# A graph network layer on one core: the first stage's weight centring moved to ScalarE, and pair sums of 17 edge chunks moved to GpSimd

## The reference

```python
xn = layernorm(x)
# graph part: sum, max and mean of the edges of each destination
out1 = segment_sum(edge_attr, dst);  out2 = segment_max(edge_attr, dst);  out3 = out1 / max(cnt, 1)
g = relu(concat([xn, out1, out2, out3, u]) @ W1 + b1) @ W2 + b2 + xn
# linear attention
q, k, v = split(xn @ W_qkv + b_qkv, 3)
q = q - mean(q);  k = k - mean(k)
k2 = l2norm_over_nodes(k*k / (sum(k*k) + 1e-7));  q2 = l2norm(q*q / (sum(q*q) + 1e-7))
m = (v + q2 @ (k2^T v) / sqrt(N)) @ W_out + b_out
x = x + g + m
# last network on the half of the nodes with the largest router weight
x = x + scatter(idx, (gelu(xs @ w1 + fb1) @ w2 + fb2) * w_sel) + layernorm(x)
```

## Time and profile before

| | |
|---|---|
| median of three runs | 1211.26 us (1210.34 to 1219.01) |
| the profiled execution's own time | 1217.11 us |
| its span, from first to last instruction | 1215.4 us |
| TensorE's mean granted clock over the span | 0.917 of full |
| VectorE busy over the span | 1011.2 us, 83% |
| TensorE busy over the span | 1062.9 us, 87% |
| GpSimd busy over the span | 465.4 us, 38% |

### The profile page before, as it was taken

The page is one execution under the profiler, slowest core; times in us unless marked ns, Lnnn a source line. Parts: engine busy times, 40 slices in busy tenths (PEclk is TensorE's granted clock), DMA queues, the critical chain, the costliest instruction groups (busy, mean ns, idle before and its releaser), DMA issues.

```text
span 1215.4 us, 15786 instructions
## 1 busy us (share of the span) xinstructions
PE 1062.9 (87%) x4570; PEld 763.7 (63%) x4570; DVE 1011.2 (83%) x2419; ACT 482.8 (40%) x1421; POOL 465.4 (38%) x341
## 2 busy tenths in 40 slices
PE   3198999999998367769999999999999967799996
PEld 1044555555554245447888888888888863588885
DVE  6899999999999999847988888988888566566672
ACT  3345777567762124412332233332233331333430
POOL 0078850888300002367565444565441000223411
PEclk9588999999997679869999999999999985699997
DMA  9879999999997899652443332443331130111100
GB/s 313 309 276 349 354 359 355 345 364 349 356 322 297 301 397 390 248 163 73 139 150 119 127 130 82 150 143 123 124 115 50 47 112 0 36 38 47 55 23 20
DMA packets 96013, 235.53 MB, mean 194 GB/s; under 512 B 13703, under 2 KB 68764, under 8 KB 89682
## 3 DMA queue, kind: packets, MB, share of 16 engines
q1 hardware_dynamic: 49890, 156.61, 35.0%
q10 hardware_dynamic: 31248, 44.71, 10.3%
q0 software_dynamic: 14816, 33.53, 9.9%
HBM read 154.25 MB, written 80.55 MB: 193 GB/s over the span
## 4 chain that ended last, share of the span: by engine, by line
PE 49%; POOL 3%; DVE 3%; issue 2%; DMA 1%; another core or an unknown queue 0%; ACT 0%; DVEq 0%; POOLq 0%
PE psR L67 5%; PE psC L67 5%; PE psQ L56 5%; PE psQ L57 5%; PE psKx L57 5%; PE psQ L58 5%; PE psKx L56 5%; PE psKx L58 5%; PE psR L68 3%; PE psC L68 2%; POOL graw L460 2%; PE psT L2012 1%; POOL grow L485 1%; PE psQ L2033 1%; PE psKx L2033 1%
## 5 line engine op out<-in xcount | busy, mean ns | idle before, releaser
L460 POOL DMA_INDIRECT graw<-in_edge_attr,ic x98 | 143.4, 1464 | 74.8 <-DVE ob L966 39.2
L963 DVE SCALAR_TENSOR_TENSOR ob<-ob,mQ,mx 128x96 f32<-128x96 f32 x392 | 122.3, 312 | 4.7 <-issue 0.4
L966 DVE SCALAR_TENSOR_TENSOR ob<-ob,kQ,xb 128x96 f32<-128x96 f32 x392 | 122.0, 311 | 0.0
L635 POOL DMA_INDIRECT near<-ends_d,blki x49 | 89.2, 1821 | 76.8 <-DVEq L872 62.2
L635 POOL DMA_INDIRECT near<-in_dst,rowi x49 | 87.8, 1792 | 57.8 <-DVEq L881 43.1
L1692 ACT ACTIVATE hT_hi<-psQ 128x512 fp32r<-128x512 f32 (+1 forms) x52 | 29.8, 574 | 185.0 <-PE psQ L2033 160.4
L1834 PE MATMUL psQ<-Wqk,xT 128*128 128x512 f32 (+1 forms) x196 | 102.3, 646 | 0.0
L951 DVE TENSOR_TENSOR xb<-xb 128x1536 f32<-128x1536 f32 x49 | 86.1, 1758 | 1.7
L949 DVE TENSOR_TENSOR mx<-xb 128x1536 f32<-128x1536 f32 x49 | 85.5, 1746 | 0.9
L729 POOL DMA_INDIRECT out_x<-zo,lst x25 | 24.4, 977 | 113.3 <-DVE zo L1384 113.3
L1692 ACT ACTIVATE hT_hi<-psKx 128x512 fp32r<-128x512 f32 (+1 forms) x52 | 29.7, 573 | 91.6 <-PE psKx L2033 83.8
(11 more groups left out here) (497 smaller groups left out, 3234.5 us busy)
## 6 DMA issues: line engine op xcount, KB each, us to landing
xb<-in_edge_attr SPq DMA_DIRECT2D x49, 1536.0 KB
scan_d<-ob SPq DMA_DIRECT2D x49, 768.0 KB
yrow_d<-yr SPq DMA_DIRECT2D x48, 132.0 KB
xg<-in_x ACTq DMA_DIRECT2D x12, 512.0 KB
xT_d<-xT ACTq DMA_DIRECT2D x12, 512.0 KB
base_d<-dcur ACTq DMA_DIRECT2D x12, 512.0 KB
qT_d<-qT ACTq DMA_DIRECT2D x12, 512.0 KB
out_x<-xres SPq DMA_DIRECT2D x48, 128.0 KB
```

What stands on the lines that cost most here:

```text
L460: nc.gpsimd.indirect_dma_start(out=to.rearrange("p i f -> p (i f)"), out_offset=None, in_=raw_v, in_offset=bass.IndirectOffsetOnAxis(ap=ic ...
L635: nc.gpsimd.indirect_dma_start(out=near[:, t, :], out_offset=None, in_=table, in_offset=bass.IndirectOffsetOnAxis(ap=rows[:, t:t + 1], axi ...
L963: nc.vector.scalar_tensor_tensor(o[:, q, 0:EF], prev[:, 0:EF], mQ[:, bass.ds(c * TQ + q, 1)], mx[:, q, 0, :], ALU.min, ALU.max).then_inc(s ...
L966: nc.vector.scalar_tensor_tensor(o[:, q, EF:AGG], prev[:, EF:AGG], kQ[:, bass.ds(c * TQ + q, 1)], X[:, q, 0, :], ALU.mult, ALU.add).then_i ...
```

## The change

Three things are changed together.

1. **Centring on ScalarE.** `centre_weights` on VectorE is gone. ScalarE does it with 12 activations: six that make minus the mean through an accumulator, six that add it. VectorE keeps the splitting (`query_bias`), now ahead of `variances`; `bias_row` stands behind chunk 0. `bqs`, `brow` and `one_r` have 128 partitions, cleared by GpSimd, and the bias matmuls have 128 rows in place of 2.
2. **Pair sums on GpSimd.** For chunks 30 to 46 (`PAIRS`) the pair sums are made by GpSimd (`pair_sums`), each when the chunk's pair maxima are done. VectorE makes the pair maxima of chunk c+1 inside chunk c, behind a wait for that chunk's load.
3. **Places.** `NORM` has smaller chunk numbers, the attention's factors come after chunk 35 in place of 39, `ends_of_segments` after 38 in place of 39, the graph network's weights are loaded from chunk 39 in place of 40. The product of `Eend` stands behind the fourth attention group; the tail parts, and ScalarE's `weights(GROUPS)`, stand later.

In the diff `pair_sums` is in GpSimd's list, `pair_maxima` and the lines on `PAIRS` after it in VectorE's, the loop over `centred` in ScalarE's.

```diff
+            PAIRS = range(30, 47)
+            def quarters(b):
+                return xb[b][:, :, :, :].rearrange("p q (h two) f -> p q h two f", two=2)
...
+                def pair_sums(chunks):
+                    for c in chunks:
+                        xp = quarters(c % XB)
+                        pool.wait_ge(s_tree, TREE[c, "max1"])
+                        nc.gpsimd.tensor_tensor(xp[:, :, :, 0, :], xp[:, :, :, 0, :], xp[:, :, :, 1, :], ALU.add).then_inc(s_pair, 1)
+                pair_sums(range(PAIRS[0], 44))
                 pool.wait_ge(s_idx, 1)
...
+                pair_sums(range(44, PAIRS[-1] + 1))
                 early(0, s_g0r)
...
+                def pair_maxima(c):
+                    xp = quarters(c % XB)
+                    dve.wait_ge(s_load[c % XB], c // XB * 16 + 16)
+                    if c in PAIRS:
+                        dve.wait_ge(s_max, (c - 1) * TQ + 1)
+                    nc.vector.tensor_tensor(mxs[c % 2][:, :, :, :], xp[:, :, :, 0, :], xp[:, :, :, 1, :], ALU.max).then_inc(s_tree, 1)
...
+                    if c not in PAIRS:
+                        xp = quarters(b)
+                        pair_maxima(c)
+                        dve.wait_ge(s_tree, TREE[c, "max1"])
+                        nc.vector.tensor_tensor(xp[:, :, :, 0, :], xp[:, :, :, 0, :], xp[:, :, :, 1, :], ALU.add).then_inc(s_tree, 1)
+                    if c + 1 in PAIRS:
+                        pair_maxima(c + 1)
...
+                    if c in PAIRS:
+                        dve.wait_ge(s_pair, c - PAIRS[0] + 1)
...
-                NORM = {5: 0, 7: 1, 10: 2, 13: 3, 16: 4, 18: 5, 21: 6, 24: 7, 26: 8, 29: 9, 32: 10, 34: 11, 35: 12}
+                NORM = {4: 0, 6: 1, 9: 2, 11: 3, 14: 4, 16: 5, 19: 6, 21: 7, 24: 8, 26: 9, 29: 10, 32: 11, 33: 12}
...
+                act.wait_ge(s_wload, 16 * 8)
+                for w_, m_, o_ in centred:
+                    nc.scalar.activation(o_, w_, ACT.Copy, scale=-1.0 / NF, accum_out=m_).then_inc(s_cw, 1)
+                for i, (w_, m_, o_) in enumerate(centred):
+                    act.wait_ge(s_cw, i + 1)
+                    nc.scalar.activation(w_, w_, ACT.Identity, bias=m_).then_inc(s_cw, 1)
+                act.wait_ge(s_bw, 2)
+                act.dma_start(brow[1:2, :].bitcast(f32), brow_l[0:1, :].bitcast(f32)).then_inc(s_row, 16)
+                act.wait_ge(s_wq, 1)
+                act.dma_start(bqs[1:2, :].bitcast(f32), bqs_l[0:1, :].bitcast(f32)).then_inc(s_row, 16)
                 act.wait_ge(s_ln, 1)
                 nc.scalar.sqrt(sd[:, :], va[:, :]).then_inc(s_sqrt, 1)
...
-                    nc.tensor.matmul(o, one_r[0:2, 0:rows], bqs[0:2, :], start=True, stop=False)
+                    nc.tensor.matmul(o, one_r[:, 0:rows], bqs[:, :], start=True, stop=False)
```

More of the change, by code:

```diff
@@ L354, in build @@
             s_xs = [sem(f"s_xs{i}") for i in range(4)]
-            s_run = sem("s_run")
-            s_diag = sem("s_diag")
+            s_cw = sem("s_cw")
+            s_pair = sem("s_pair")
             s_ct = sem("s_ct")
@@ L455, in build @@
                     9: ("h5", "l8", "l9"), 10: ("l10", "l11"), 12: ("t0", "t1", "t2", "t3")}
+            PAIRS = range(30, 47)
+            TREE = {}
+            for c_ in range(CHUNKS):
+                own = () if c_ in PAIRS else ((c_, "max1"), (c_, "add1"))
+                ahead = ((c_ + 1, "max1"),) if c_ + 1 in PAIRS else ()
+                for k_ in own + ahead + ((c_, "max2"), (c_, "add2")):
+                    TREE[k_] = len(TREE) + 1
+            def quarters(b):
+                return xb[b][:, :, :, :].rearrange("p q (h two) f -> p q h two f", two=2)
             def gather_raw(e, nt, rows, done):
@@ L800, in row_ends, with query_bias @@
                     dve.sem_inc(s_cbc, 1)
[L802 to L820, removed]
+                def query_bias():
+                    dve.wait_ge(s_cw, 12)
+                    dve.wait_ge(s_id, 9)
                     step(nc.vector.tensor_copy(one_r[0:2, :], ones[0:2, :]), False)
@@ L981, in _ @@
                 edge_chunk(0, 0, 0)
+                bias_row()
                 stats_quarter(1)
                 stats_quarter(2)
+                stats(GROUPS, 1, LAST, xs[0], s_xs[0], 64)
+                query_bias()
                 variances()
-                centre_weights()
-                bias_row()
                 deviations()
@@ L1653, in attention_rows @@
                         fetch(g + 4)
-                for g in range(GROUPS + 1):
+                for g in range(GROUPS):
                     attention_rows(g, g % 4, g // 4 * 16)
                     weights(g)
+                attention_rows(GROUPS, 0, GROUPS // 4 * 16)
                 for e in range(4):
@@ L1843, in base @@
                     o = psC[0:rows, 0:NF]
-                    nc.tensor.matmul(o, one_r[0:2, 0:rows], brow[0:2, :], start=True, stop=False)
+                    nc.tensor.matmul(o, one_r[:, 0:rows], brow[:, :], start=True, stop=False)
                     for c in range(KF):
@@ L1933, in _, with starts_of_segments @@
                 ins.then_inc(s_pt, 1)
-                pe.wait_ge(s_end, 1)
-                nc.tensor.matmul(psR[:, 0:TILES], shift[:, :], Eend[:, :], start=True, stop=False)
-                nc.tensor.matmul(psR[:, 1:TILES], corner[:, :], Eend[:, 0:TILES - 1], start=False, stop=True).then_inc(s_t, 1)
                 pe.wait_ge(s_at, 6 + KF)
+                def starts_of_segments():
+                    pe.wait_ge(s_end, 1)
+                    nc.tensor.matmul(psKx[1][:, 0:TILES], shift[:, :], Eend[:, :], start=True, stop=False)
+                    nc.tensor.matmul(psKx[1][:, 1:TILES], corner[:, :], Eend[:, 0:TILES - 1], start=False, stop=True).then_inc(s_t, 1)
                 def low_part(i):
@@ L1945, in low_part @@
                     pe.wait_ge(s_min, 4)
+                    if i == 3:
+                        pe.wait_ge(s_idx, 1)
                     if i >= 4:
@@ L1981, in _ @@
                     attention(g, g % 4, g // 4 * 16 + 16)
+                    if g == 3:
+                        starts_of_segments()
                     weights(g)
@@ L1994, in _ @@
                 ins.then_inc(s_t, 1)
-                tail_part(2)
-                tail_part(3)
+                for i in range(4):
+                    tail_part(i)
                 def node_stage():
```

63 lines of the change are left out of this document (28 added, 35 removed).

## The result

The kernel before took 1215.04 us (median of 4 runs), the changed one 1234.37 us (1229.56 to 1236.35): the ratio is 1.015, with an interval from 1.0111 to 1.0189. A second comparison of the same two kernels on another occasion gave 1.0161 (1.0133 to 1.0188), 1234.19 us against 1214.13. The change makes the kernel some 19 us slower. A few executions in this document were far longer whatever the kernel (1389.2 us for the kernel before, 1373.5 in experiment 1, 3494 and 5585 in experiment 6), and the ratios leave them out.

What follows compares the result with a forecast made beforehand. VectorE bounds the scan, busy 178.68 of 182.82 us from chunk 30 on. Pair sums +27, start -3 and key norms +2 made +26 us on a median of 1211.3: 1237 us, range 1226 to 1251.

Steps and rivals of the forecast that it cites:

- the side that had 0.87: Whole kernel: the change makes it slower by over 1%, chance 0.87.
- Both engines at one time: Scan: VectorE's two-SBUF-input instructions and a reading GpSimd instruction exclude each other; what GpSimd takes, VectorE loses.
- rival (a): Pair sums in the scan: the engines share after all, scan steps keep their usual length, 1184 us; chance 8%.
- Part 1, +27 us: Pair sums on GpSimd: 3.3 us lost, 1.7 freed, net +1.6 us a chunk over 17 chunks.
- Rival (b): GpSimd's pair sums: addition dearer on runs of 96 elements, 4.2 us each, 12 us more, 1249 us; chance 13%.
- Rival (d): GpSimd's pair sums: addition cheaper or partly beside one-input instructions, 0.5 us less a chunk, 1228 us; chance 8%.
- Part 2, -3.2 us: Start of the scan: with centring on ScalarE, chunk 1 starts at 51.6 us and not 54.8.
- this path ends last: Start of the scan: ScalarE's DMA issue, table load and root end at 49.5 us, later than the variances at 48.85.
- Part 3, the key norms, +2 us: Earlier key norms: VectorE might wait for ScalarE's squares, bounds 0 and 7 us, taken as +2.
- cost no more columns: Bias matmuls with 128 rows: no added columns; could bring TensorE's clock, up to 3.4 us gained each time.
- waits don't add: Key norms: VectorE waits 7 us ahead of group 9's norm, less for other groups, without summing.
- Rival (c): Key norms in the scan: they wait in full, +5 us more, 1242 us; chance 14%.

Runs made afterwards that it cites:

- experiment 1: The changed kernel with all pair sums on VectorE again and no pair maxima ahead: 1209.08 us, ratio 0.9953 to the kernel before.
- experiment 6: The changed kernel with GpSimd's pair sums in chunks 30 to 37 alone, 8 in place of 17: 1221.96 us, ratio 1.0067 to the kernel before.
- experiments 3: The changed kernel with GpSimd clearing the 1536 elements in place of adding them, pair sums left out: 1189.53 us in one execution.
- Experiment 4: The changed kernel with GpSimd adding two flat halves of the chunk in place of every second run of 96: 1232.63 us in one execution.
- experiment 5: The changed kernel with GpSimd copying the 1536 elements (one SBUF input) in place of adding two: 1200.24 us in one execution.
- experiment 10: The changed kernel with all pair sums on VectorE and ScalarE's table load early, right behind the centring: 1205.87 us in one execution.
- experiment 9: The changed kernel with all pair sums on VectorE and bias products of 2 rows, not 128: 1217.66 us, ratio 1.0021 to the kernel before.
- experiment 2: The kernel before with only the pair sums of chunks 30 to 46 on GpSimd and pair maxima ahead: 1237.39 us, ratio 1.0196.

## Why the prediction was right, and where it was not

The forecast was 1237 us with a range of 1226 to 1251, and the time was 1234.4, on the side that had 0.87. That it came out within 3 us is partly luck, since two errors offset each other: it stood on a median of 1211.3 for the kernel before, which more runs put at 1214 to 1216, and its sum of +26 was +19.5 (1.0161 x 1214 less 1214).

- **Both engines at one time.** Right in kind: experiments 3, 4 and 5 show that VectorE's two-input instructions wait for a GpSimd instruction that reads, and not for one that only writes. So rival (a) falls. The Trainium skill's rule in "SBUF — State Buffer", section "Who interferes with whom", says the same of reading and writing, and the traces agree (0.95 us for L970 under a clear, 4.20 under an addition).
- **Part 1, +27 us.** It was +22.5. Of the two figures in it, the loss of 3.3 us a chunk was 3.1 (3.25 and 3.0 in the two patterns), and the 1.7 us freed were 1.8. The prediction had both patterns, except that it saw the second as a wait of VectorE for the sums; in fact a scan step is held. Both errors go one way, 0.28 us a chunk: that is the term that was mis-sized. Most of it comes from the length of the addition, 3.5 us in the prediction (2.2 ns an element) and 3.3 in the trace, once it has its turn.
- **Rival (b), runs of 96 elements.** Experiment 4: no difference. Rival (d), 0.5 us less a chunk, is nearest to what happened, at a little over half its size.
- **Part 2, -3.2 us.** 29.5 and 30.2 us against 32.6 and 32.5: -2.7 on average, and -3.1 over all eleven traces with the new start (28.2 to 30.7). The step "this path ends last" held, and by the right size: 49.5 - 48.85 = 0.6 us by the prediction's times, 0.7 in the trace. Of that the table load makes only 0.3, which experiment 10 shows.
- **Part 3, the key norms, +2 us.** This step failed. TensorE's chain did start 4 to 5 us sooner (first query product at 55.3 us, 60.2 before), but VectorE never waited ahead of a key norm, and the reason is one that the prediction denied: it said that the padded rows "cost no more columns", could bring only the clock, and "lie inside the busy part". They take 0.5 to 0.9 us off each tile's products at the same clock (from one query bias to the next, without transposes between, 206.64 to 209.90 is 3.26 us, against 196.70 to 200.84, 4.14 us, in the kernel before; with the key product behind, 3.54 against 4.03), so that TensorE's chain ran ahead. Without them the earlier norms would have cost 10.7 us (experiment 9), more than the upper bound of 7, and not as the prediction had it: it said that "waits don't add", but there are three, 4.9, 2.9 and 3.0 us, ahead of the norms of groups 5, 7 and 9, and they add up. Rival (c) therefore fell by luck, not by its argument.
- **Behind the scan, nothing.** It was -1.8 us on average, -0.3 to -3.3 between single executions. I had given no term for it. The attention work ended at 486 and not at 501 to 504 us, but TensorE's last weight pieces stood behind the scan in any case, so that little came of it. That is not the padded rows' doing alone: with the factors in their new place and two rows it ended at 486 too (experiment 9), with padded rows as well at 473 (experiment 1), both without GpSimd's pair sums, and in the old place it ended at 505 (experiment 2).

## What to carry to other kernels

Before moving an elementwise operation with SBUF inputs from a saturated VectorE to an idle GpSimd, compare GpSimd's own duration (3.3 us) with what VectorE is freed of (1.8 us): beside two-input instructions the move pays only if the first is smaller, however idle GpSimd looks. The copy of experiment 5, which holds VectorE for 1.0 to 1.3 us, is on the other side of that line. A change made of several parts deserves one run for each: here one part cost 22.5 us, and another, which looked like tidying, was worth 8 in time (1217.7 against 1209) and 11 at the scan's end, beside norms that had been moved ahead; what it is worth with the norms in their old places was not run. Small matmuls over a few rows between full ones were dearer here than they look; read the idle time ahead of weight loads, not only the matmuls' lengths.

## What the runs showed of the hardware that I had not expected

A matmul over 2 rows between matmuls over 128 delays the ones around it: 1.91 against 1.31 us for the same four matmuls at a granted clock of 1.00, and 0.76 us without a weight load ahead of the 2-row one. GpSimd's recorded length under a busy VectorE includes its wait for its turn: 4.09 or 4.96 us for one addition of 3.3, and 2.13 or 3.00 for one copy that holds VectorE for 1.27 or 1.04. And the two patterns came in the same order in both executions of the changed kernel, with the held instructions within 0.1 us of the same place: the exclusion is as regular as the rest of the schedule.
